# Last projection in four passes instead of two halves, its successor's factors and weights prepared inside it, and the feed-forward without loops

## The chip, the cores and the metric

One core of one Trainium2 chip runs the whole program. The metric is the device time of one execution in microseconds (us): 3321.41 us for the kernel before, the median of 3 runs (3314.15 to 3323.13). The change touches the last two of the kernel's stages.

## What is computed

The reference is a two-layer gated cross-attention block over 2048 tokens (4 sequences of 512) of width 512. Only its end matters here:

```python
x = x + jnp.tanh(g_xattn[1]) * _L1_xattn_ref(_layernorm(x), ...)   # ends in a projection
x = x + jnp.tanh(g_ffn[1]) * _L1_ffn_ref(_layernorm(x), w_gate_up, w_down, norm_weight)

# the end of _L1_xattn_ref: catq is 2048 x 4096, wproj 512 x 4096
return jnp.einsum('bsi,oi->bso', catq, wproj) * (proj_in_scale * proj_w_scale)

def _L1_ffn_ref(x, w_gate_up, w_down, norm_weight):
    def rmsnorm(x, weight, eps=1e-5):
        return x * jax.lax.rsqrt(jnp.mean(x * x, -1, keepdims=True) + eps) * weight
    def activation_quant(x):
        scale = 127.0 / jnp.clip(jnp.max(jnp.abs(x), -1, keepdims=True), 1e-05, None)
        return jnp.clip(jnp.round(x * scale), -128, 127) / scale
    def weight_quant(w):
        scale = 1.0 / jnp.clip(jnp.mean(jnp.abs(w)), 1e-05, None)
        return jnp.clip(jnp.round(w * scale), -1, 1) / scale
    def bitlinear(x, w):
        return jnp.einsum('bsh,oh->bso', activation_quant(x), weight_quant(w))
    gate, up = jnp.split(bitlinear(rmsnorm(x, norm_weight), w_gate_up), 2, axis=-1)
    return bitlinear(jnp.square(jax.nn.relu(gate)) * up, w_down)       # hidden width 1408
```

The weights of the feed-forward are made ternary (-1, 0, 1), which needs the mean magnitude of the whole matrix first.

## The kernel before

The two stages stand in `l1_output_and_ffn` (L2825). Tokens are handled in 16 tiles of 128. Each stage has its own buffers and semaphores and ends with a barrier of all engines. PE, DVE, ACT, POOL and SP are TensorE, VectorE, ScalarE, GpSimd and SyncE; each runs its own list of instructions in order and waits on semaphores.

**Projection, `l1_output` (L2837).** The contraction of 4096 is cut into 32 slices (k). The tokens go in two halves of 8 tiles, each tile with a PSUM bank (`acc0` to `acc7`). For each half and slice, SP loads `cat16` (128 x 1024, bf16), ACT turns it into fp32r (L2901), and PE makes two products for each tile, with the high and the low part of the weight slice (L2917, L2918). In the first half SP also loads the weight slice `w_raw`, DVE makes `w_hi` (L2940) and POOL `w_lo` (L3004); both stay for the second half. The order of SP's first loads is: two scale constants (L2879, L2880), then cat and weight in turn (L2886, L2889). SP loads the residual `x3` (4 MB, L2891) at slice 24 of the first half. When a half is done, DVE handles its tiles one by one: scaled addition to `x3` (L2991), which frees the bank, then mean and variance (L2994, L2996). In the second half PE waits at each bank's first product for that tile's L2991.

Beside this the ternary weights are made: POOL issues the loads of 12 parts of the raw weights (`t_raw`, L3016) in the first 24 slices, DVE sums magnitudes (L2951). Between the two halves' tiles DVE has `limits` and then 12 parts of `ternary` (L2976, L2979), each of them loaded again (L3027) and stored to DRAM (`wguq`, `wdq`, L3030) by POOL. POOL's last act in the stage is to wait for these stores.

**Feed-forward, `l1_ffn` (L3038).** SP loads `w_gate_up` in four pieces (L3105), `norm_w` (L3106) and `w_down` (L3107). POOL works out, for all 16 tiles together, the factor and bias of the double normalisation (11 dependent operations, L3281 to L3291, two of them powers); ACT and DVE wait for all 11. Then each tile goes through: ACT `centre` (xa, L3183), POOL `weigh` (xb, L3261), DVE `scale` (a maximum over 512 and two small steps, L3197 to L3202), `round_add` (xr, L3206), `round_sub` (xi, L3211), PE transposes (pX), ACT copy (hT, L3164), then four quarters of PE `gate_up` (L3134), ACT relu and square (L3170, L3173), DVE `hidden` (L3218); then DVE `hidden_scale` (the long maximum over 1408, L3223, and three small steps), `hidden_round` (L3236), `hidden_int` (L3241), PE transposes (pT, L3142), ACT copy (qT, L3178, L3179), PE `down` (L3153), DVE `residual` (L3247), SP store. The order on each engine is set by `pipeline` (L31): a stage with lag l handles item s - l in step s, the stages of a step in the order of the list; there are 64 items, four quarters for each tile, and `at(q, f)` runs f in quarter q alone. Steps before the largest lag and the last ones are written out, those between are a loop of 8 steps (2 tiles) on every engine. PE's gate_up of quarter i waits until `hidden` of quarter i - 2 is done (two banks).

## Time and profile before

| | |
|---|---|
| median of 3 runs | 3321.41 us |
| profiled execution, its own time | 3319.0 us |
| its span, first to last instruction | 3317.3 us |
| TensorE's mean granted clock | 0.959 |
| busy: PE, DVE, ACT, POOL | 2961.9, 2408.8, 2094.6, 1360.3 us |
| projection: first product to end of the last | 2861.5 to 3102.9 us |
| feed-forward: first gate product to the end | 3131.7 to 3317.3 us |

Times in the rows are microseconds from the start of the span, durations too unless marked ns. PE's matmuls overlap, so the distance between two starts is what one costs; PEld is the loading of its stationary operand. An operand's name carries the prefix `k_` in these stages. In brackets behind a row: how long the engine sat idle before it, and what released it.

### The profile page before, as it was taken

The page shows a single profiled execution, that of the slowest core. Times are in us where ns is not written, and L with a number is a line of the kernel's source. Part 1 is how long each engine was busy: PE and PEld are TensorE (multiplying, and loading weights), DVE is VectorE, ACT ScalarE, POOL GpSimd, SP SyncE. Part 2 cuts the span into 40 slices and gives each one's busy share as a digit, 9 for nine tenths or more (in the row PEclk, how much of TensorE's full clock was granted, in tenths as well). Part 3 has the DMA queues.
Part 4 walks back from the last instruction along what each step waited for, and adds up shares of the span by engine and source line. Part 5 has one row for each costly group of instructions (what it writes and reads, how often), then busy time and mean ns, then how long its engine had stood idle before and what let it go on. Part 6 is the DMA issues. An engine that isn't in the chain of part 4 may idle for free. (4 is left out here: it accounts for less than half of the span.)

```text
span 3317.3 us, 57690 instructions
## 1 busy us (share of the span) xinstructions
PE 2961.9 (89%) x15542; PEld 2354.9 (71%) x15542; DVE 2408.8 (73%) x4802; ACT 2094.6 (63%) x4247; POOL 1360.3 (41%) x1667
## 2 busy tenths in 40 slices
PE   6849899588899969979999899999999999799677
PEld 4636666477788857758787688888888888678444
DVE  6759999656676658767666189999999999534387
ACT  3448888331566636556666488888888888322255
POOL 3400000413000048246676277777777776331131
PEclk9979999799899989989999999999999999899899
DMA  5776564413877759865666523222233221566200
GB/s 184 245 158 157 140 157 109 120 48 137 278 262 263 232 159 300 208 180 154 175 175 200 187 88 95 93 91 76 90 95 93 93 93 45 173 234 206 71 23 29
DMA packets 403247, 490.88 MB, mean 148 GB/s; under 512 B 36388, under 2 KB 251828, under 8 KB 403092
## 3 DMA queue, kind: packets, MB, share of 16 engines
q1 hardware_dynamic: 391140, 440.31, 44.8%
q0 software_dynamic: 11952, 48.78, 4.2%
q8 instruction: 63, 1.03, 0.1%
q14 instruction: 92, 0.75, 0.1%
HBM read 312.69 MB, written 176.31 MB: 147 GB/s over the span
## 5 line engine op out<-in xcount | busy, mean ns | idle before, releaser
L2814 POOL TENSOR_SCALAR h_probs<-h_exp,h_rowsum_inv 128x512 f32<-128x512 f32 x512 | 357.5, 698 | 273.9 <-PE h_pT L2662 256.4
L2742 DVE TENSOR_REDUCE h_neg_max<-h_scores 128x1 f32<-128x512 f32 x512 | 349.4, 682 | 141.8 <-PE h_scores L2654 141.4
L2704 ACT ACTIVATE h_exp<-h_scores,h_neg_max 128x512 f32<-128x512 f32 x512 | 356.0, 695 | 108.8 <-DVE h_neg_max L2742 100.6
L2755 DVE TENSOR_TENSOR h_probsT_lo<-h_pT,h_probsT_hi 128x512 fp32r<-128x512 f32 x512 | 348.3, 681 | 0.0
L2662 PE MATMUL h_pT<-ident,h_probs 128*128 128x128 f32 x2048 | 306.2, 272 | 0.9 <-POOL h_probs L2814 0.8
L2662 PEld LDWEIGHTS h_pT<-ident,h_probs 128*128 128x128 f32 x2048 | 253.1, 139 | 69.9 <-POOL h_probs L2814 2.3
L2713 ACT CAST h_probsT_hi<-h_pT 128x512 fp32r<-128x512 f32 x512 | 301.1, 588 | 0.9 <-PE h_pT L2662 0.9
L2917 PE MATMUL k_acc<-k_w_hi,k_cat 128*128 (+1 forms) x512 | 202.4, 395 | 19.5 <-ACT k_cat L2901 16.2
L817 ACT ACTIVATE b_probs<-b_scores,b_neg_max 128x512 f32<-128x512 f32 x256 | 180.5, 705 | 39.9 <-DVE b_neg_max L845 39.6
L845 DVE TENSOR_REDUCE b_neg_max<-b_scores 128x1 f32<-128x512 f32 x256 | 173.7, 679 | 38.7 <-PE b_scores L768 38.7
L2677 PE MATMUL h_pO<-h_probsT_hi,n_lo 128*128 128x512 f32 x512 | 201.5, 393 | 0.0
L2918 PE MATMUL k_acc<-k_w_lo,k_cat 128*128 (+1 forms) x512 | 201.3, 393 | 0.0
L2901 ACT CAST k_cat<-k_cat 128x1024 fp32r<-128x1024 bf16 x64 | 67.3, 1051 | 183.4 <-PE k_acc L2918 170.1
L826 ACT CAST b_probsT_hi<-b_pT 128x512 fp32r<-128x512 f32 x256 | 151.6, 592 | 44.5 <-PE b_pT L776 44.4
L2513 DVE TENSOR_TENSOR g_normed<-g_pQ,g_rstd 128x512 f32<-128x512 f32 x160 | 110.3, 689 | 95.2 <-PE g_pT L2418 95.2
L2543 POOL TENSOR_TENSOR g_rstd<-g_var_eps,neg_half 128x4 f32<-128x4 f32 x160 | 172.0, 1075 | 13.3
L852 DVE TENSOR_TENSOR b_probsT_lo<-b_pT,b_probsT_hi 128x512 fp32r<-128x512 f32 x256 | 174.0, 680 | 1.4 <-issue 1.4
L2801 POOL TENSOR_TENSOR n_lo<-n_raw,n_hi_second 128x512 fp32r<-128x512 f32 x128 | 165.3, 1292 | 0.0
L2462 ACT ACTIVATE g_out<-g_pT,head_ln_b,head_ln_w 128x512 f32<-128x512 f32 x160 | 124.5, 778 | 61.1 <-DMA lnT<-g_out 60.4
L776 PE MATMUL b_pT<-ident,b_probs 128*128 128x128 f32 x1024 | 159.9, 279 | 3.5 <-DVE b_probsT_lo L852 2.3
L768 PE MATMUL b_scores<-b_k_stack,b_q_stack 128*128 128x512 f32 x256 | 124.1, 486 | 40.9 <-DMA b_k_stack<-qk 39.2
L776 PEld LDWEIGHTS b_pT<-ident,b_probs 128*128 128x128 f32 x1024 | 122.6, 142 | 48.2 <-issue 8.9
(439 smaller groups left out, 9135.4 us busy)
## 6 DMA issues: line engine op xcount, KB each, us to landing
e_w_raw<-in_w SPq DMA_DIRECT2D x24, 1792.0 KB, 8.0
lnT<-g_out SPq DMA_DIRECT2D x160, 256.0 KB, 2.4
n_raw<-lnT SPq DMA_DIRECT2D x64, 512.0 KB, 5.2
e_w_raw<-in_w SPq DMA_DIRECT2D x24, 896.0 KB, 9.6
b_q_stack<-qk SPq DMA_DIRECT2D x64, 256.0 KB, 7.3
b_k_stack<-qk SPq DMA_DIRECT2D x64, 256.0 KB, 9.2
xq<-f_out SPq DMA_DIRECT2D x16, 1024.0 KB, 7.1
n_raw<-lnT SPq DMA_DIRECT2D x64, 256.0 KB, 5.3
```

Source lines behind the costliest of these rows:

```text
L776: last = nc.tensor.transpose(pT[r % TB][:, k], Pr[:, r % 4, bass.ts(k, P)], g["ident"][:])
L817: nc.scalar.activation(Pr[:, r % 4], pS[r % SB][:], ACT.Exp, bias=nmax[:, r % 4:r % 4 + 1], accum_out=rsum[:, h, q:q + 1]).then_inc(exp_do ...
L852: nc.vector.tensor_tensor(PTl[:, h, :, bass.ts(q, P)], pT[r % TB][:], PTh[:, h, :, bass.ts(q, P)], ALU.subtract).then_inc(lo_done.sem, 1)
L2662: last = nc.tensor.transpose(pT[r % 4][:, k], Pn[:, r % 4, bass.ts(k, P)], g["ident"][:])
L2677: nc.tensor.matmul(pO[h][:], vl, PTh[:, br * HPG + h, k], start=False, stop=(k == QT - 1)).then_inc(o_mm.sem, 1)
L2704: nc.scalar.activation(Pr[:, r % 4], pS[r % 2][:], ACT.Exp, bias=nmax[:, r % 4:r % 4 + 1], accum_out=rsum[:, r % 4:r % 4 + 1]).then_inc(ex ...
L2713: nc.scalar.copy(PTh[:, br * HPG + h, :, bass.ts(q, P)], pT[r % 4][:]).then_inc(hi_done.sem, 1)
L2742: v.tensor_reduce(nmax[:, r % 4:r % 4 + 1], pS[r % 2][:], axis=AX, op=ALU.max, negate=True).then_inc(nmax_done.sem, 1)
L2755: v.tensor_tensor(PTl[:, br * HPG + h, :, bass.ts(q, P)], pT[r % 4][:], PTh[:, br * HPG + h, :, bass.ts(q, P)], ALU.subtract).then_inc(lo_ ...
L2814: nc.gpsimd.tensor_scalar(Pn[:, r % 4], Pr[:, r % 4], rinv[:, r % 4:r % 4 + 1], 1.0, ALU.mult, ALU.mult).then_inc(norm_done.sem, 1)
L2917: nc.tensor.matmul(pA[j][:], lhsT, Wh[:, k].rearrange("p a d -> p (a d)"), start=first, stop=False)
L2918: ins = nc.tensor.matmul(pA[j][:], lhsT, Wl[:, k].rearrange("p a d -> p (a d)"), start=False, stop=last)
```

## The change

The projection (`l1_output`) goes through the tokens in four passes of 4 tiles. Passes 0 and 1 are interleaved slice by slice, so that each weight slice still serves 8 tiles when it comes; passes 2 and 3 follow one after the other, on banks 0 to 3 and 4 to 7. An item is one slice of one pass (128 x 512 of cat): 128 items, 8 products each, all written out without a loop. cat has 8 buffers before ACT's conversion and 4 behind. SP's first load is a weight slice, the scale constants come behind the second cat, `x3` at item 32 (slice 16 of the interleaved passes). At item 64 SP waits for all `w_lo` and loads `norm_w` into a free weight buffer. At item 112, in the middle of pass 3, SP waits for the ternary stores and loads `w_gate_up` for the feed-forward; the ternary work's buffers lie in that same memory. DVE's order is unchanged in kind: tiles 0 to 7, limits, 12 ternary parts, tiles 8 to 15, where tiles 8 to 11 now belong to pass 2 and 12 to 15 to pass 3.

After its last store POOL works out the output constants and, once 12 tiles have their variance, the row factors of tiles 0 to 11 (4 operations with one power, the two normalisations being joined algebraically). Those of tiles 12 to 15 are made in the feed-forward, behind POOL's first `weigh`. Nobody waits for them before `centre` of tile 12. `w_down` is still loaded at the start of the feed-forward.

In the feed-forward every engine's list is written out in full. `centre` moves from quarter 0 to quarter 3 of the tile before, behind the hT copy on ACT; `weigh`, `scale`, `round_add` and `round_sub` move with it: DVE has `scale` between `hidden_round` and the second `hidden`, `round_add` behind `hidden_int`, and `round_sub` behind `residual`. All other lags grow by one. The diff, cut:

```diff
+    TP = 4
+    PASSES = NT // TP
+    N = PASSES * CK
+    def item(n):
+        return (n % 2, n // 2) if n < 2 * CK else divmod(n, CK)
+    UW, UC, UX = 4, 8, 4
+    X3, MV, Wr = shared.x3, shared.meanvar, shared.w_raw
...
-    Cb = m.sb("cat16", [P, U, HT * P], BF16)
-    Ct = m.sb("cat", [P, 2, HT * P], F32R)
+    Cb = m.sb("cat16", [P, UC, TP * P], BF16)
+    Ct = m.sb("cat", [P, UX, TP * P], F32R)
...
+    flat = shared.w_gate_up[:].rearrange("p k c -> p (k c)")
+    Tr = flat[:, 0:4 * F1].bitcast(F32).rearrange("p (a c) -> p a c", a=2)
+    Lt = flat[:, 4 * F1:5 * F1]
+    Tq = flat[:, 5 * F1:7 * F1].rearrange("p (a c) -> p a c", a=2)
...
+        def load_cat(n):
+            p, k = item(n)
+            if n >= UC:
+                sp.wait_ge(c_conv, n - UC + 1)
+            sp.dma_start(Cb[:, n % UC], t["cat"][k * P:(k + 1) * P, p * TP * P:(p + 1) * TP * P]).then_inc(c_in[n % UC], 16)
+        def load_w(k):
+            if k >= UW:
+                sp.wait_ge(w_lo, k - UW + 1)
+            sp.dma_start(Wr[:, k % UW], t["wprojT"][k * P:(k + 1) * P, :]).then_inc(w_in[k % UW], 16)
+        for n in range(N):
+            if n < 2 * CK and n % 2 == 0:
+                load_w(n // 2)
+            load_cat(n)
+            if n == 1:
+                sp.dma_start(sc[:, 0:1], t["proj_in_scale"].partition_broadcast(P)).then_inc(s_in, 16)
+                sp.dma_start(sc[:, 1:2], t["proj_w_scale"].partition_broadcast(P)).then_inc(s_in, 16)
+            if n == CK:
                 sp.dma_start(X3[:], t["x2"].rearrange("(n p) d -> p n d", p=P)).then_inc(x_in, 16)
-        segments(sp, [CK, CK], U, [(load, 0)], straight_end=CK // 2)
+            if n == 2 * CK:
+                sp.wait_ge(w_lo, CK)
+                sp.dma_start(shared.norm_w, t["norm_w"].partition_broadcast(P)).then_inc(shared.nw_in, 16)
+            if n == 3 * CK + CK // 2:
+                for r in range(2):
+                    sp.wait_ge(t_stored[r], 16 * NP // 2)
+                for k in range(KT):
+                    sp.dma_start(shared.w_gate_up[:, k], t["wguq"][k * P:(k + 1) * P, :]).then_inc(shared.gu_in, 16)
     @block.scalar
     def _(act):
-        def convert(seg, i, r):
-            n = i * U + r
-            act.wait_ge(c_in[r], i * 16 + 16)
-            act.wait_ge(mm.sem, mm.free(n))
-            nc.scalar.copy(Ct[:, r % 2], Cb[:, r]).then_inc(c_conv.sem, 1)
-        segments(act, [CK, CK], U, [(convert, 0)])
+        for n in range(N):
+            act.wait_ge(c_in[n % UC], 16 * (n // UC + 1))
+            if n >= UX:
+                act.wait_ge(mm, n - UX + 1)
+            nc.scalar.copy(Ct[:, n % UX], Cb[:, n % UC]).then_inc(c_conv, 1)
     @block.tensor
     def _(pe):
...
+        for n in range(N):
+            p, k = item(n)
+            pe.wait_ge(c_conv, n + 1)
+            if p == 0:
+                pe.wait_ge(w_lo, k + 1)
+            for j in range(TP):
+                bank = pA[p % 2 * TP + j]
+                if k == 0 and p >= 2:
+                    pe.wait_ge(x3_done, (p - 2) * TP + j + 1)
+                lhsT = Ct[:, n % UX, bass.ts(j, P)]
+                nc.tensor.matmul(bank[:], lhsT, Wh[:, k], start=(k == 0), stop=False)
+                ins = nc.tensor.matmul(bank[:], lhsT, Wl[:, k], start=False, stop=(k == CK - 1))
+                if k == CK - 1 and j < TP - 1:
+                    ins.then_inc(acc_done, 1)
+            ins.then_inc(mm, 1)
...
+        def tile(n):
+            p, j = divmod(n, TP)
+            if j < TP - 1:
+                dve.wait_ge(acc_done, p * (TP - 1) + j + 1)
+            else:
+                dve.wait_ge(mm, max(p + 1, 2) * CK - (p == 0))
...
+        for k in range(CK):
+            high(k)
+            if k % 2 and k // 2 < NP:
+                abs_sum(k // 2)
+        dve.wait_ge(summed, NP)
+        v.tensor_reduce(tot[:, 0:1], asum[:, 0:GP], axis=AX, op=ALU.add).then_inc(t_link, 1)
+        v.tensor_reduce(tot[:, 1:2], asum[:, GP:NP], axis=AX, op=ALU.add).then_inc(t_link, 1)
+        dve.wait_ge(s_in, 32)
+        v.tensor_tensor(gs[:, 0:1], sc[:, 0:1], sc[:, 1:2], ALU.mult).then_inc(s_done, 1)
+        dve.wait_ge(s_done, 1)
+        v.tensor_tensor(gs[:, 1:2], gs[:, 0:1], g["tanh_gates"][:, 1:2], ALU.mult).then_inc(s_done, 1)
...
-            if n == HT:
+            if n == 2 * TP:
                 limits()
                 for part in range(NP):
                     ternary(part)
...
+            tile(n)
...
+        shared.chain(pool, nc.gpsimd.tensor_scalar(shared.out_const[:, 0:1], g["w_mean"][:, 1:2], 1.0 / INT8, 1.0, ALU.mult, ALU.mult))
+        shared.chain(pool, nc.gpsimd.tensor_tensor(shared.out_const[:, 1:2], shared.out_const[:, 0:1], g["tanh_gates"][:, 3:4], ALU.mult))
+        pool.wait_ge(mv_done, shared.EARLY)
+        shared.row_factors(nc, g, pool, 0, shared.EARLY)
...
-        return i * 2 + r // CH, r // CH, r % CH
+        n, c = divmod(i * N + r, CH)
+        return n, n % 2, c
...
-        for k in range(KT):
-            sp.dma_start(Wg[:, k], t["wguq"][k * P:(k + 1) * P, :]).then_inc(gu_in, 16)
-        sp.dma_start(nw[:], t["norm_w"].partition_broadcast(P)).then_inc(nw_in, 16)
...
-        pipeline(sp, N, U, [(at(3, store), 0)])
+        pipeline(sp, N, N, [(at(3, store), 0)])
...
-        pipeline(pe, N, U, [(gate_up, 8), (down_part, 15), (at(3, h_transposes), 11), (at(3, x_transposes), 4)])
+        pipeline(pe, N, N, [(gate_up, 9), (down_part, 16), (at(3, h_transposes), 12), (at(3, x_transposes), 5)])
...
         def centre(n, b):
+            if n == shared.EARLY:
+                act.wait_ge(shared.rows_done, 2)
             act.wait_ge(xb.sem, xb.free(n))
...
-        act.wait_ge(pre, 11)
-        pipeline(act, N, U, [(at(3, qT_copy), 12), (relu_square, 8), (at(3, hT_copy), 4), (at(0, centre), 0)])
+                                 bias=sbias[:, bass.ds(n, 1)], scale=srow[:, bass.ds(n, 1)]).then_inc(xa.sem, 1)
...
-        dve.wait_ge(pre, 11)
-        pipeline(dve, N, U, [(at(3, hidden_scale), 9), (at(3, hidden_round), 10), (at(3, hidden_int), 11),
-                             (at(3, residual), 16), (at(1, round_add), 4), (at(2, round_sub), 4), (at(3, scale), 0),
-                             (hidden, 8)])
+        pipeline(dve, N, N, [(at(3, hidden_scale), 10), (at(3, hidden_round), 11), (at(3, hidden_int), 12),
+                             (at(3, residual), 17), (at(3, round_add), 4), (at(3, round_sub), 5), (at(3, scale), 3),
+                             (hidden, 9)])
...
             pool.wait_ge(xa.sem, xa.done(n))
+            if n == 0:
+                pool.wait_ge(shared.nw_in, 16)
             pool.wait_ge(xr.sem, xr.free(n))
-            nc.gpsimd.tensor_tensor(Xb[:, b], Xa[:, b], nw[:], ALU.mult).then_inc(xb.sem, 1)
+            nc.gpsimd.tensor_tensor(Xb[:, b], Xa[:, b], nw, ALU.mult).then_inc(xb.sem, 1)
+            if n == 0:
+                shared.row_factors(nc, g, pool, shared.EARLY, NT)
...
-        var = MV[:, :, 1:2].rearrange("p n a -> p (n a)")
-        steps = (
-            lambda: nc.gpsimd.tensor_scalar(row[:, 0], var, EPS, 0.0, ALU.add, ALU.add),
...
-        for k, step in enumerate(steps):
-            step().then_inc(pre, 1)
-            pool.wait_ge(pre, k + 1)
-        pool.wait_ge(nw_in, 16)
-        pipeline(pool, N, U, [(at(0, weigh), 0), (at(3, cubes), 1), (at(3, out_factor), 10)])
+        pipeline(pool, N, N, [(at(3, weigh), 2), (at(3, cubes), 3), (at(3, out_factor), 11)])
...
+    def row_factors(self, nc, g, pool, a, b):
+        mean, var = (self.meanvar[:, a:b, j:j + 1].rearrange("p n a -> p (n a)") for j in range(2))
+        c = slice(a, b)
+        self.chain(pool, nc.gpsimd.tensor_scalar(self.row[:, 0, c], var, 1.0 + EPS, EPS * EPS, ALU.mult, ALU.add))
+        self.chain(pool, nc.gpsimd.tensor_tensor(self.factor[:, c], self.row[:, 0, c], g["neg_half"][:, 0:b - a], ALU.pow))
+        self.chain(pool, nc.gpsimd.tensor_tensor(self.row[:, 1, c], mean, self.factor[:, c], ALU.mult))
+        nc.gpsimd.tensor_scalar(self.bias[:, c], self.row[:, 1, c], -1.0, 0.0, ALU.mult, ALU.add).then_inc(self.rows_done, 1)
```

## Rows read from the trace of the kernel before

**Rows 1.** Busy time by stretch: us, PE, PEld, DVE, ACT, POOL, PEclk, DMA share, GB/s
```profile
2980.00:3000.00 20.00, 16.71 (x57) 11.51 (x56) 15.19 (x28) 3.69 (x4) 2.50 (x4) 0.83 0.35 108
3103.00:3127.00 24.00, 0.00 (x0) 0.00 (x0) 9.07 (x19) 1.52 (x2) 8.02 (x12) 0.59 0.39 145
```

**Rows 2.** Timeline of the projection's start: start, length, engine, line, operation
```profile
2851.69 0.34 SPq L2879 DMA_DIRECT2D k_scales<-in_proj_in_scale  x1
2853.43 0.34 SPq L2889 DMA_DIRECT2D k_w_raw<-in_wprojT  x1
...
2861.48 0.76 PE L2917 MATMUL k_acc<-k_w_hi,k_cat 128*128 128x512 f32 x1 [16.22 <-ACT k_cat L2901]
```

**Rows 3.** The tile k_acc, and the timeline near the end of the first half
```profile
L2917 PE MATMUL k_acc<-k_w_hi,k_cat x512: 389/389/794, 2861.5 to 3102.2; 128*128 x128, 128*128 128x512 f32 x43
...
2975.86 1.05 ACT L2901 CAST k_cat<-k_cat 128x1024 fp32r<-128x1024 bf16 x1 [2.58 <-PE k_acc L2918]
2976.42 0.75 DVE L2991 SCALAR_TENSOR_TENSOR k_x<-k_acc,k_gated_scale,k_x 128x512 f32<-128x512 f32 x1 [13.69 <-PE k_acc L2918]
```

**Rows 4.** Timeline from the projection's last tiles to the first gate product
```profile
3099.72 0.75 DVE L2991 SCALAR_TENSOR_TENSOR k_x<-k_acc,k_gated_scale,k_x 128x512 f32<-128x512 f32 x1 [50.51 <-PE k_acc L2918]
...
3112.30 0.18 DVE L2996 BATCH_NORM_AGGREGATE k_meanvar<-k_bnstat 128x2 f32<-128x6 f32 x1
3113.53 0.31 POOL L3281 TENSOR_SCALAR k_row_scale<-k_meanvar 128x16 f32<-128x16 f32 x1 [63.47 <-POOLq L121]
...
3115.49 2.17 SPq L3105 DMA_DIRECT2D k_w_gate_up<-wguq  x4
...
3122.33 1.52 ACT L3183 ACTIVATE k_xa<-k_x,k_row_bias,k_row_factor 128x512 f32<-128x512 f32 x2 [25.64 <-POOL k_row_bias L3291]
3126.92 2.49 POOL L3261 TENSOR_TENSOR k_xb<-k_xa,k_norm_w 128x512 f32<-128x512 f32 x2 [4.62 <-DMA k_norm_w<-in_norm_w]
...
3129.02 0.15 DVE L3200 TENSOR_SCALAR k_act_step<-k_amax 128x1 f32<-128x1 f32 x1
...
3131.70 1.36 PE L3134 MATMUL k_gate<-k_w_gate_up,k_hT 128*128 128x352 bf16 x4 [0.68 <-ACT k_hT L3164]
```

**Rows 5.** Timeline of one tile in the feed-forward's loop, from gate to gate
```profile
3196.24 0.77 PE L3134 MATMUL k_gate<-k_w_gate_up,k_hT 128*128 128x352 bf16 x4 [0.94 <-ACT k_hT L3164]
...
3199.57 1.79 POOL L3261 TENSOR_TENSOR k_xb<-k_xa,k_norm_w 128x512 f32<-128x512 f32 x1 [7.41 <-ACT k_xa L3183]
...
3200.15 1.50 DVE L3206 TENSOR_SCALAR k_xr<-k_xb,k_act_scale 128x512 f32<-128x512 f32 x1
...
3204.23 0.67 DVE L3197 TENSOR_REDUCE k_amax<-k_xb 128x1 f32<-128x512 f32 x1
...
3206.71 1.62 DVE L3223 TENSOR_REDUCE k_amax<-k_hidden 128x1 f32<-128x1408 f32 x1
...
3207.16 0.77 PE L3134 MATMUL k_gate<-k_w_gate_up,k_hT 128*128 128x352 bf16 x4 [0.83 <-ACT k_hT L3164]
```

**Rows 6.** The same near the end, written out, with neither weigh nor scale
```profile
3283.39 0.77 PE L3134 MATMUL k_gate<-k_w_gate_up,k_hT 128*128 128x352 bf16 x4 [0.68 <-ACT k_hT L3164]
...
3285.82 0.52 DVE L3218 TENSOR_TENSOR k_hidden<-k_relu,k_up 128x352 f32<-128x352 f32 x1 [0.41 <-ACT k_relu L3173]
...
3287.12 0.48 DVE L3206 TENSOR_SCALAR k_xr<-k_xb,k_act_scale 128x512 f32<-128x512 f32 x1
...
3289.05 0.79 PE L3142 MATMUL k_pT<-ident,k_hidden_int 128*128 128x128 bf16 x11 [0.17 <-DVE k_hidden_int L3241]
...
3293.04 0.77 PE L3134 MATMUL k_gate<-k_w_gate_up,k_hT 128*128 128x352 bf16 x4 [0.68 <-ACT k_hT L3164]
```

**Rows 7.** Loads of the projection, KB and median us to landing; POOL's last store
```profile
k_w_raw<-in_wprojT SPq DMA_DIRECT2D x32, 256.0 KB, 4.4
...
k_x<-x SPq DMA_DIRECT2D x1, 4096.0 KB, 14.1
...
3049.51 0.55 POOL L3030 DMA_DIRECT2D wdq<-k_ternary  x1 [5.25 <-DVE k_ternary L2979]
```

227 lines of the change are left out of this document (84 added, 143 removed).

## The prediction, made before the changed kernel ran

> **What bounds the kernel now.** I read the busy time by stretch first, for where PE stands idle; then the timeline at the edges of the two stages; then one tile of the feed-forward. The projection is bound by PE: 1024 products [rows 3], and ACT's conversions follow PE at 1.05 + 2.58 = 3.63 us for 16 products, so one costs 0.2267 us and all 232.1 us. PE takes from 2861.48 to 3102.9, 241.4 us. Of the 9.3 us above, 1.6 are eight first products at half clock (0.425 us in place of 0.227, the granted clock still low), the rest, 7.7, lies between the halves: DVE needs about 1.6 us for a tile (8 tiles in 3112.48 - 3099.72 = 12.8, [rows 4]), PE only 0.453, so PE waits at the banks, and the granted clock of that stretch is 0.83 [rows 1]. Then PE is idle from 3102.9 to the feed-forward: DVE's tiles to 3112.48, POOL's factors until ACT starts at 3122.33, the wait for norm_w, which stands behind 2.8 MB of weights in SP's queue, until 3126.92, and the chain to the first gate at 3131.70 [rows 4]. Then 16 tiles, one each 10.92 us [rows 5], with DVE's xr on the path: 1.50 us while POOL weighs, 0.48 without [rows 5, 6].
>
> **The change part by part.**
>
> Start. Before the first weight slice SP issues two scales and one cat; it starts at 2851.69 and comes to the slice at 2853.43 [rows 2]. Now the slice is first: 1.7 us at least. From its issue to PE's first product passed 8.05 us, of which its cast and POOL's subtraction are about 1.9, so it landed after 6.1; its like land after 4.4 in the median [rows 7]. If the slice alone in front does too, 1.7 more. Bounds: 1.7 gained, and 4.5 (also without the start flags). I take 3.0. The second slice may still be late, but eight slow products stand before it.
>
> Middle. DVE starts tile 0 at the same place, 3.1 us before the last product of the interleaved passes [rows 3]. Bank j is free 0.75 + 1.6j us later (0.8, 2.3, 3.9, 5.5). PE is there at 3.2 + 0.45j, as a whole item of the other four banks (8 x 0.2267 = 1.81 us) lies between: 3.2, 3.6, 4.1, 4.5. Only tile 3 is late, by 1.0 us; pass 3's banks are free long before. A wait this short should leave the clock up. Gained 7.7 - 1.2 = 6.5; at worst the clock drops for some us (4 gained). Between passes 2 and 3 nothing waits: DVE is in the ternary parts, but those banks are not used.
>
> Tail of the projection. DVE has four tiles behind the last products in place of eight: 4 x (1.58 - 0.45) = 4.5 us less. DVE is free by then: its ternary ends some 10 us into pass 3.
>
> Front of the feed-forward. Old: from DVE's end 3112.48 to the gate, 19.2 us. New: barrier 1.05 (to POOL's 3113.53), centre 0.76, weigh 1.25, small hand-offs 0.3, then from the end of the first weigh to the gate as before 3131.70 - 3128.17 = 3.5: in sum 6.9. Gained 12.3. Bounds: if ACT's flag comes only with SP's first issue (3115.49, behind all start flags) 10.4; nothing is left that could give more than 13. The 11 POOL operations are covered by pass 3; those for tiles 12 to 15, at most the old 4 us, run while PE makes tile 0 and delay POOL's second weigh, which DVE needs only some 7 us later.
>
> Feed-forward. The tile period where everything is written out, POOL silent and DVE without scale, is 3293.04 - 3283.39 = 9.65 us, and there the pT transposes wait 0.17 us for hidden_int [rows 6]: the chain gate, relu, first hidden, rounding, xr, second hidden, hidden_int, pT, qT, down, pX, hT, gate sets it. In the new order xr leaves that stretch (0.5) and scale enters it: 0.67 [rows 5] and two small steps of about 0.15 [rows 4] with hand-offs, 1.1 us. So 9.65 + 1.1 - 0.5 = 10.25. Where is POOL? centre ends 0.8 us after the gate, weigh runs from 0.8 to 2.1, the long maximum from -0.45 to 1.2 [rows 5], its small steps to 1.8, rounding begins at 2.9 (hidden at 2.43, [rows 6]). So weigh meets only the small steps. Three cubes behind scale on POOL may touch hidden_int for 0.2. 15 periods: 15 x 10.25 = 153.8 against 3293.04 - 3131.70 = 161.3, 7.5 us gained. Bounds: 0 (period stays) and 16.6 (15 x 9.65). The last tile is as before.
>
> Do the small steps wait for weigh? The first act_step, a scalar operation on one column, ran at 3129.02 for 0.15 us in the middle of two weighs that held POOL from 3126.92 to 3129.41 [rows 4], whereas the wide xr took 1.50 beside one. So I cost it at nothing. The Trainium skill, "SBUF — State Buffer", section "Who interferes with whom", says that DVE's tensor_scalar may take the port pair shared with GpSimd, exclusively, and that whoever issues first blocks the other wholly; that fits xr, and taken literally the small steps of the hidden scale too would wait for weigh; by the row they do not, and by the page's word the sum would be some 5 us smaller, which is in rival 1.
>
> DMA. SP's wait at item 112: SP gets there when PE has done item 100, 9 us into pass 3. The last ternary store is issued at 3049.51 in the old time, 3046.5 in the new, lands about 5 later (4.4 for 256 KB, [rows 7]), 16 us into pass 3, which starts near 3035.3. Then four issues, and the weights take at most 11.4 us (3115.49 to 3126.92, norm_w behind them included, [rows 4]); cat 113 lands near 28. PE has work until 17 x 1.81 = 30.8. So it is hidden, with 2 to 3 us to spare. x3 comes at slice 16, beside t_raw loads, where before it came after them: 14.1 us [rows 7] against a stock of 12 items, 21.8 us. Hidden too, with about as much to spare.
>
> **Sum.** 3.0 + 6.5 + 4.5 + 12.3 + 7.5 = 33.8. The profiled execution took 3319.0 (span 3317.3), 2.4 below the median shown: 3319.0 - 33.8 = 3285.2, I say 3285 us.
>
> **Rivals.** A difference under 0.3% (10 us) is about what a measurement of this kernel cannot tell from none.
>
> 1. The tile period hardly falls: weigh blocks the small steps (they end at 2.7, hidden moves from 2.4 to 2.8, 0.4 x 14 = 5.6 us), or the new chain through weigh, scale and second hidden is tighter than I drew it, up to the old 10.92. For it: pT already waits for hidden_int. Against: act_step. Time 3285 + 5 to 8 = 3290 to 3293. Chance 0.17.
> 2. PE starves in the projection, at item 113 or behind x3. For it: the margins are 2 to 3 us of DMA time. Against: PE never starved in the old one, x3 in it. 3 to 8 us, half clock after it included: 3288 to 3293; with rival 1 up to 3300. Chance 0.13.
> 3. It does not do what it says at the edge: ACT starts centre only after SP's start flags, and the first slice lands no sooner: 1.9 + 1.3 less, 3288. Inside my own range.
> 4. Slower than before: code written out must be fetched. The feed-forward has 16 x 58 products and as many weight loads on PE, the projection 2048. If each new block of code stopped PE as long as a small load takes to land, 4.4 us, it would take 34 / 4.4 = 8 stops to eat the gain and 10 for a measurable loss; 15 stops give 3285 + 66 = 3351. Against: the end of the old feed-forward is written out and its only waits have names [rows 6]. It decides from 10 stops on. Chance 0.03.
>
> **How the numbers follow.** My forecast has 0.64; the cases within 0.3% (several shortfalls at once, above 3311) 0.03, rival 4 0.03. Everything else is faster by over 0.3%: 0.94. The range reaches down for a period near 9.9 and the best start (5 + 1.5 less, and some noise of the runs) to 3275, and up to rivals 1 and 2 together, 3300.
>
> **What would show it.** PE's first product near 2858.5; no wait between passes above 1.5 us and granted clock 1.00 there; projection's last product near 3093; xb starting 2 us after DVE's last variance, gate 7 us after it; k_xr at 0.48 throughout and gates 10.25 apart; PE idle on k_cat in pass 3 below 1 us. A k_xr still near 1.5, gates 10.9 apart, waits for k_cat by DMA, or idle PE put down to issue would make it wrong.

## The result and the profile after

The changed kernel took 3281.68 us (median of 4 runs, 3272.32 to 3285.97), the kernel before, on the same chip, 3320.9 us (4 runs). The ratio is 0.9881, with a 95% interval from 0.9865 to 0.9897. I had said 3285 us, between 3275 and 3300.

The profiled execution took 3272.32 us, of which the span is 3270.6. In it the stages ahead of the change, which are the same program, were 8.2 us shorter than in the profile of before, so spans can't be compared whole. I cut the time from attention's last operation on DVE (its start) to the end at four places. All experiments are read by the same cuts.

| us | to the first product | products | to DVE's end | to the first gate | first gate to the end | in all |
|---|---|---|---|---|---|---|
| before | 13.8 | 241.4 | 9.6 | 19.2 | 185.6 | 469.6 |
| after | 8.1 | 236.2 | 5.1 | 6.7 | 175.0 | 431.2 |
| gained | 5.7 | 5.2 | 4.5 | 12.5 | 10.6 | 38.4 |
| predicted | 3.0 | 6.5 | 4.5 | 12.3 | 7.5 | 33.8 |

The start, in the timeline of after (start, duration, what; the rows of before are [rows 2]):

```profile
2839.42 0.42 DVE L1789 TENSOR_TENSOR h_cat<-h_o_clipped,h_magic 128x512 bf16<-128x512 bf16 x1
...
2842.84 0.34 SPq L2890 DMA_DIRECT2D k_w_raw<-in_wprojT  x1
...
2843.35 0.65 POOL L3019 DMA_DIRECT2D k_w_gate_up<-in_wguT  x1 [12.57 <-POOLq L121]
...
2845.61 0.43 DVE L2942 CAST k_w_hi<-k_w_raw 128x512 fp32r<-128x512 f32 x1 [5.76 <-DMA k_w_raw<-in_wprojT]
...
2846.13 1.26 POOL L3011 TENSOR_TENSOR k_w_lo<-k_w_raw,k_w_hi 128x512 fp32r<-128x512 f32 x1 [2.13 <-DVE k_w_hi L2942]
...
2847.54 0.77 PE L2930 MATMUL k_acc<-k_w_hi,k_cat 128*128 128x512 f32 x1 [10.52 <-POOL k_w_lo L3011]
```

SP's first act is the slice, 3.4 us after attention's operation (5.8 before); DVE starts to cast it 2.8 us later, where before 6.1 passed from issue to cast. The load of POOL's beside it carries the name `k_w_gate_up` because the raw weights now lie in that tile.

The change of banks, in the timeline of after, and the busy time by stretch (per engine, with the number of instructions; then PE's granted clock, the DMA engines' share, GB/s):

```profile
2966.80 0.39 PE L2931 MATMUL k_acc<-k_w_lo,k_cat 128*128 128x512 f32 x1
2967.22 0.50 PE L2930 MATMUL k_acc<-k_w_hi,k_cat 128*128 128x512 f32 x1
...
2968.80 0.50 PE L2930 MATMUL k_acc<-k_w_hi,k_cat 128*128 128x512 f32 x1 [0.85 <-DVE k_x L2980]
```

```profile
2962.00:2970.00 8.00, 7.13 (x30) 5.28 (x30) 6.47 (x13) 2.25 (x4) 0.00 (x0) 1.00 0.22 67
```

Products start 0.227 us apart. Two gaps stand out: 0.42 ahead of tile 2 (0.2 late) and 1.25 ahead of tile 3 (1.0 late), 1.2 in all, and the clock stays at 1.00, where it was 0.83 at the change of halves [rows 1].

The front of the feed-forward, in the timeline of after (before: [rows 4]):

```profile
3088.70 0.18 DVE L2985 BATCH_NORM_AGGREGATE k_meanvar<-k_bnstat 128x2 f32<-128x6 f32 x1
...
3090.03 0.81 ACT L3189 ACTIVATE k_xa<-k_x,k_row_bias,k_row_factor 128x512 f32<-128x512 f32 x1 [12.80 <-SPq L152]
...
3090.93 1.26 POOL L3267 TENSOR_TENSOR k_xb<-k_xa,k_w_raw 128x512 f32<-128x512 f32 x1 [46.34 <-ACT k_xa L3189]
...
3091.58 0.38 SPq L3111 DMA_DIRECT2D k_w_down<-wdq  x1
...
3095.62 1.36 PE L3138 MATMUL k_gate<-k_w_gate_up,k_hT 128*128 128x352 bf16 x4 [0.68 <-ACT k_hT L3168]
```

The row factors are there, POOL waits for ACT alone, and only `w_down` is still to be issued. ACT starts 1.55 us ahead of SP's first issue: of the row of start flags that SP sets (L152, which the row names) it waits for its own, one of the first, and not for the rest. (`norm_w` lies in a free weight buffer, so `weigh` reads it under the name `k_w_raw`.)

A tile of the feed-forward, the same view, and all 16 xr by their line (minimum, median, maximum in ns):

```profile
3154.25 1.62 DVE L3228 TENSOR_REDUCE k_amax<-k_hidden 128x1 f32<-128x1408 f32 x1
...
3155.28 1.27 POOL L3267 TENSOR_TENSOR k_xb<-k_xa,k_w_raw 128x512 f32<-128x512 f32 x1 [4.34 <-ACT k_xa L3189]
...
3155.90 0.21 DVE L3232 TENSOR_SCALAR k_clipped_max<-k_amax,k_cube 128x1 f32<-128x1 f32 x1
...
3156.35 0.21 DVE L3236 TENSOR_SCALAR k_hidden_scale<-k_max_inv,k_cube 128x1 f32<-128x1 f32 x1
...
3158.27 0.68 DVE L3202 TENSOR_REDUCE k_amax<-k_xb 128x1 f32<-128x512 f32 x1
...
3159.67 0.89 DVE L3246 TENSOR_SCALAR k_hidden_int<-k_hidden_rounding 128x1408 bf16<-128x1408 f32 x1
...
3159.76 0.84 POOL L3278 TENSOR_TENSOR k_cube<-k_cube 128x1 f32<-128x1 f32 x1
...
3160.47 0.48 DVE L3211 TENSOR_SCALAR k_xr<-k_xb,k_act_scale 128x512 f32<-128x512 f32 x1
```

```profile
L3211 DVE TENSOR_SCALAR k_xr<-k_xb,k_act_scale x16: 478/479/485, 3093.3 to 3241.0; 128x512 f32<-128x512 f32 x16
```

POOL's weigh (3155.28 to 3156.55) lies beside the long maximum and the two small steps, and neither small step is longer for it (0.21 us each, and 0.21 again at 3246.50, where POOL is silent); xr has POOL's weigh behind it and takes 0.48 in all 16 tiles. Tiles follow at 10.07 us (10.92 and 10.99 by turns in the loop before), and the loads of the weights in pass 3 cost PE nothing: in the stretch no wait of PE for a converted `cat` is listed, nor one of ACT for a load. The nearer escape was at `x3`, behind which the load of item 33 came late for ACT (timeline of after):

```profile
2907.27 0.62 ACT L2916 CAST k_cat<-k_cat 128x512 fp32r<-128x512 bf16 x1 [3.74 <-DMA k_cat<-cat]
```

PE came to this item at 2909.91, 2.0 us after the end of its conversion; three items later, and in pass 3, a conversion ends 4.6 us ahead of its products.

### The profile page after: what moved, and what is told of

It reads as the page before. It is cut to its first block and busy times, and to the rows that moved or that the text cites. A ratio compares the mean times of both kernels' runs of the same rounds, so it can differ in the third digit from the quotient of the medians.

```text
span 3270.6 us, 57041 instructions
## 1 busy us (share of the span) xinstructions
PE 2953.2 (90%) x15542; PEld 2349.0 (72%) x15542; DVE 2395.1 (73%) x4802; ACT 2107.6 (64%) x4311; POOL 1351.6 (41%) x1666
## 5 line engine op out<-in xcount | busy, mean ns | idle before, releaser
L2930 PE MATMUL k_acc<-k_w_hi,k_cat 128*128 128x512 f32 x512 | 201.0, 393 | 11.4 <-POOL k_w_lo L3011 10.5
L2931 PE MATMUL k_acc<-k_w_lo,k_cat 128*128 128x512 f32 x512 | 200.5, 392 | 0.0
L2916 ACT CAST k_cat<-k_cat 128x512 fp32r<-128x512 bf16 x128 | 79.3, 621 | 160.2 <-PE k_acc L2931 142.8
L757 POOL DMA_DIRECT2D rows<-b_zero x16 | 8.8, 548 | 359.1 <-PE b_scores L768 358.8
```

What stands on the lines that cost most here:

```text
L2930: nc.tensor.matmul(bank[:], lhsT, Wh[:, k], start=(k == 0), stop=False)
L2931: ins = nc.tensor.matmul(bank[:], lhsT, Wl[:, k], start=False, stop=(k == CK - 1))
```

## The experiments

Here are the same cuts for every kernel that ran, with the steady distance from one tile's first gate to the next one's (half the distance of two where a loop makes them alternate). The time is that of one execution, for before, after and the last kernel a median. The stages ahead end anywhere between 2839.4 and 2852.6 us, and the kernels ran on several chips, so the cuts carry the comparison, not the time. The first column scatters from 8.1 to 9.9 us between kernels with the same start: the slice is cast 2.7 to 3.5 us after its issue, and in four of them (old order, factors late, halves, scale aside) the first product waited for ACT's conversion of cat instead, which ended up to 9.8 us after attention's operation. The product stretch scatters by some 0.9 us with the number of slow products at its head (7 to 13). The last stretch scatters with the granted clock: over the first 7.4 us from the first gate it was 0.75 to 0.82 in most kernels and 0.59 to 0.66 in five (old order, halves, POOL's load later, scale aside, xr behind hidden). Where the feed-forward is that of after, such a late clock makes the first tile 9.4 or 9.5 us long in place of 8.6 to 8.9.

| us | first product | products | DVE's end | first gate | gate to end | tile | time |
|---|---|---|---|---|---|---|---|
| before | 13.8 | 241.4 | 9.6 | 19.2 | 185.6 | 10.96 | 3320.9 |
| after | 8.1 | 236.2 | 5.1 | 6.7 | 175.0 | 10.07 | 3281.7 |
| old order, straight | 8.9 | 236.2 | 5.1 | 6.7 | 182.0 | 10.51 | 3290.9 |
| new order, loops | 8.1 | 236.8 | 5.1 | 6.7 | 181.9 | 10.65 | 3289.6 |
| factors late | 8.4 | 236.8 | 5.1 | 11.1 | 175.1 | 10.07 | 3285.1 |
| loads late | 8.5 | 236.2 | 5.1 | 18.9 | 175.0 | 10.07 | 3292.8 |
| halves of eight | 9.9 | 241.5 | 9.6 | 6.7 | 177.0 | 10.07 | 3285.8 |
| start order of before | 13.5 | 237.0 | 5.1 | 6.7 | 175.1 | 10.07 | 3287.9 |
| the same, POOL's load later | 10.7 | 237.2 | 5.1 | 6.7 | 176.8 | 10.07 | 3288.9 |
| wait at item 96 | 8.2 | 255.4 | 5.1 | 6.7 | 175.0 | 10.07 | 3303.6 |
| scale aside | 9.4 | 236.1 | 5.1 | 6.7 | 169.2 | 9.65 | 3280.8 |
| x early | 8.8 | 236.5 | 5.1 | 6.7 | 163.8 | 9.33 | 3270.7 |
| fourth gate first | 8.6 | 236.2 | 5.1 | 6.7 | 151.3 | 8.73 | 3258.1 |
| xr behind hidden | 8.2 | 237.1 | 5.1 | 6.7 | 150.8 | 8.45 | 3257.3 |

**The order or the straight code?** The feed-forward changed in two ways. One run takes the new order away, one the straight code.

```diff
-        pipeline(dve, N, N, [... (at(3, round_add), 4), (at(3, round_sub), 5), (at(3, scale), 3), (hidden, 9)])
-        pipeline(pool, N, N, [(at(3, weigh), 2), (at(3, cubes), 3), (at(3, out_factor), 11)])
+        pipeline(dve, N, N, [... (at(1, round_add), 4), (at(2, round_sub), 4), (at(3, scale), 0), (hidden, 8)])
+        pipeline(pool, N, N, [(at(0, weigh), 0), (at(3, cubes), 1), (at(3, out_factor), 10)])
```

> Everything as in the changed kernel, but the feed-forward's engines go in the order of before (centre and weigh at a tile's first step, scale beside the last hidden of the tile before, round_add and round_sub at steps 1 and 2), still written out straight. Theory (xr beside POOL's weigh was the price): k_xr takes 1.50 us again in all tiles where POOL weighs, the tile period is 9.65 + (1.50 - 0.48) = 10.67 us and the 15 periods from the first gate to gate 15 about 158 to 160 us, 9 to 10 more than the 149.5 of the changed kernel. Rival (the loop with its register work was the price, the order is worth little): periods near 10.1, 15 of them at 150 to 152 us. The rest of the program as in the changed kernel.

```diff
-        pipeline(pe, N, N, [(gate_up, 9), ...])
+        pipeline(pe, N, U, [(gate_up, 9), ...])      # U = 8 steps to a turn of the loop, on every engine
```

> The new order of the feed-forward, but in loops of 8 steps as before in place of straight code. Theory: the order carries most of the gain and the loop costs about 0.25 us a tile (10.92 in the old loop against 9.65 + 1.02 = 10.67 worked out for straight code), so k_xr stays at 0.48, periods are about 10.3 us and 15 of them 153 to 154 us (149.5 in the changed kernel). Rival (straight code carries it): periods 10.7 or more, 160 us and over. Second rival (a loop costs nothing): 149.5 to 150.5.

xr of the first and of the second kernel, by their line:

```profile
L3211 DVE TENSOR_SCALAR k_xr<-k_xb,k_act_scale x16: 479/1495/1499, 3104.9 to 3258.4; 128x512 f32<-128x512 f32 x16
```

```profile
L3211 DVE TENSOR_SCALAR k_xr<-k_xb,k_act_scale x16: 478/480/487, 3103.6 to 3258.2; 128x512 f32<-128x512 f32 x16
```

The old order brings the 1.50 us back, in straight code too, and a tile takes 10.51; the new order in loops has xr at 0.48 and 10.65. Each alone, against before, gives 3.6 or 3.7 us of the stage; both together give 10.6. Neither theory was whole: over the 15 periods (a period is the distance from one tile's first gate to the next one's) I had the order at 9 to 10 us and it is 7.6 (157.1 against 149.5), and the loop at 4 and it is 7.0 (156.5). In the column from gate to end they are 7.0 and 6.9.

These totals hold something that is not order. In the second tile the granted clock fell for some 3.4 us in the profile of before (0.57 in 3148 to 3152) and in that of the old order (0.57 in 3123 to 3127), and not in after or in the new order in loops. That tile took 12.04 us in before, over a steady 10.96, and 11.71 in the old order, over 10.51. So some 1.1 us of the 10.6 and 1.2 of the 7.0 went with the clock; between two kernels with the feed-forward of after such a fall made 1.2 us too (11.2 against 10.1, below). The steady distances are free of it: 10.96, 10.51, 10.65 and 10.07.

Where the loop's time goes is seen along the chain of one tile, 10.71 us in the loop and 10.07 in straight code. For example, from the end of the reduction `k_amax` to the start of `k_act_step` there are 0.13 us in the loop, 0.03 in straight code.

```profile
3171.99 0.68 DVE L3202 TENSOR_REDUCE k_amax<-k_xb 128x1 f32<-128x512 f32 x1
...
3172.80 0.15 DVE L3205 TENSOR_SCALAR k_act_step<-k_amax 128x1 f32<-128x1 f32 x1
```

The rows are the loop's; after has 3158.27 + 0.68 = 3158.95 and `k_act_step` at 3158.98. Counted from the tile's first gate, the first hidden part starts at 2.71 (2.43 in straight code), `k_act_step` at 4.82 (4.44), `k_hidden_int` at 5.55 (5.13), qT's copy at 7.39 (6.89), hT's at 10.00 (9.43) and the next gate at 10.71 (10.07). The operations last as long in both; the 0.64 us are hand-offs, each up to 0.20 us longer, and 0.28 of them lie ahead of the first hidden part.

**The front: factors or loads?** One kernel computes constants and all row factors at the feed-forward's start, one issues the loads there.

```diff
-        pool.wait_ge(mv_done, shared.EARLY)
-        shared.row_factors(nc, g, pool, 0, shared.EARLY)
...
+        shared.row_factors(nc, g, pool, 0, NT)       # in l1_ffn, ahead of POOL's pipeline
```

> The two constants and the row factors of all 16 tiles are computed on POOL at the feed-forward's start in place of behind the twelfth tile; the loads stay early. Theory (loads and factors lay beside each other before, and either alone keeps its own part of the 12.5 us): one power of 128x16 at 2.93 us (half the old factors' 5.86), three short operations and two constants, 0.2 to 0.3 each with hand-offs of 0.1, 4.5 to 5 us in all: the first gate 11.2 to 11.8 us after DVE's end in place of 6.7. Rival (POOL's factors are hidden beside something else): 6.7 to 8 us.

```diff
-            if n == 3 * CK + CK // 2: ... w_gate_up; if n == 2 * CK: ... norm_w
+        for k in range(KT):                          # in l1_ffn, ahead of w_down
+            sp.dma_start(Wg[:, k], t["wguq"][k * P:(k + 1) * P, :]).then_inc(shared.gu_in, 16)
+        sp.dma_start(nw, t["norm_w"].partition_broadcast(P)).then_inc(shared.nw_in, 16)
```

> w_gate_up in four loads, norm_w and w_down are issued at the feed-forward's start in the order of before; the row factors stay early. Theory (of the 12.5 us at the front, the late norm_w alone would take nearly all): SP's first issue comes 2.7 us after DVE's end, norm_w lands 11.4 later as before, then 4.8 to the first gate: the gate 18.5 to 19 us after DVE's end (6.7 in the changed kernel, 19.2 before), the time 12 us longer, although the row factors are ready. Rival (part of the factors' 8.8 us on POOL was on the path beside the loads): gate at 10 to 15 us.

The timeline of the kernel with late loads:

```profile
3098.33 0.81 ACT L3186 ACTIVATE k_xa<-k_x,k_row_bias,k_row_factor 128x512 f32<-128x512 f32 x1 [12.80 <-SPq L152]
...
3102.02 0.44 SPq L3107 DMA_DIRECT2D k_w_raw<-in_norm_w  x1
...
3111.39 1.26 POOL L3264 TENSOR_TENSOR k_xb<-k_xa,k_w_raw 128x512 f32<-128x512 f32 x1 [57.87 <-DMA k_w_raw<-in_norm_w]
...
3116.08 1.36 PE L3135 MATMUL k_gate<-k_w_gate_up,k_hT 128*128 128x352 bf16 x4 [0.68 <-ACT k_hT L3165]
```

The loads came as expected and the factors 0.1 us under their range. Factors late cost 4.4 us (6.7 to 11.1; it is the new form of four operations, the old eleven were not tried with early loads), loads late 12.2 (6.7 to 18.9): of the 12.5 gained, 0.3 is left for the factors once the loads are late. They lay beside each other, and whoever had moved only the factors would have seen next to nothing.

**Passes of four or straight code?**

```diff
-    TP = 4
+    TP = 8          # two halves, pass p in the same eight banks; cat 4 deep, x3 at slice 16
```

> The last projection in two halves of eight tiles again, with the changed kernel's straight code, early loads and row factors (eight of them early). Theory (banks freed at 1.6 us a tile against 0.45 of PE are what the passes save): PE waits at the banks between the halves some 7 us and its granted clock drops, products take 241 to 243 us in place of 236.2, and DVE ends 9.6 us after the last product in place of 5.1: together 10 us more, and 1 to 2 more for the eight row factors left for the feed-forward, if at all. Rival (straight code or the new start of the loads brought the 5 us of the projection, not the passes): products at 236 to 238 us with only the 4.5 at the tail lost.

Busy time of this kernel around the change of halves:

```profile
2969.00:2990.00 21.00, 17.80 (x63) 13.00 (x64) 16.14 (x27) 3.91 (x4) 2.49 (x4) 0.84 0.42 143
```

The stretch at the change of halves has the granted clock of before (0.84, [rows 1]: 0.83), the products take 241.5 us and the tail 9.6: straight code gives the projection nothing, the passes all of it. The rest of the gate-to-end column (2.0 more) is not the eight factors. The kernel with POOL's load later has 1.8 more and no such factors; in both the granted clock rose late in the first tile and fell again in the second (for 3122.5 to 3126.5 here, 0.58, behind 1.7 us in which PE waited for `k_hidden_int`), and that tile took 11.2 and 11.3 us. The same view of that stretch:

```profile
3122.50:3126.50 4.00, 3.92 (x21) 2.65 (x23) 1.14 (x3) 1.73 (x3) 0.42 (x2) 0.58 0.00 0
```

After and the four other kernels with its feed-forward have the same wait of 1.7 us without the fall. Why it fell in two executions of the seven stays open.

**The start.**

```diff
+            if n == 0:
+                sp.dma_start(sc[:, 0:1], ...); sp.dma_start(sc[:, 1:2], ...)
+            load_cat(n)
+            if n < 2 * CK and n % 2 == 1:
+                load_w(n // 2)
```

> SP issues the two scales and a cat load ahead of the first weight slice, as before; the rest as changed. Theory (the place of the slice in SP's queue is the gain at the start): from the last DVE operation of attention to the first product 1.7 to 5 us more than the 8.1 to 9.4 us of the changed kernel's kind, 10 to 13.8. Rival (the dropped start flags or the load's own scatter made the 5.7 us): 8 to 9.5 us, no difference.

The timeline of this start:

```profile
2848.64 0.42 DVE L1789 TENSOR_TENSOR h_cat<-h_o_clipped,h_magic 128x512 bf16<-128x512 bf16 x1
...
2852.04 0.34 SPq L2894 DMA_DIRECT2D k_scales<-in_proj_in_scale  x1
...
2852.55 0.65 POOL L3019 DMA_DIRECT2D k_w_gate_up<-in_wguT  x1 [12.53 <-POOLq L121]
...
2854.04 0.43 SPq L2890 DMA_DIRECT2D k_w_raw<-in_wprojT  x1
...
2860.22 0.43 DVE L2942 CAST k_w_hi<-k_w_raw 128x512 fp32r<-128x512 f32 x1 [11.16 <-DMA k_w_raw<-in_wprojT]
```

The old order alone gives 13.5 us, nearly the 13.8 of before. But the slice is issued only 2.0 us later (5.4 after attention's operation in place of 3.4) and lands 3.4 us later still (6.2 from issue to cast in place of 2.8). What differs is who is ahead: POOL's load of 704 KB stands 1.5 us ahead of the slice here (1.8 before), 0.5 us behind it in after. So one more run put POOL's load behind its first subtraction and left the rest.

```diff
-                load(part, part)
+                if k: load(part, part)
             low(k)
+            if k == 0: load(0, 0)
```

> The start order of before (scales and one cat ahead of the first weight slice), and POOL's first load of the ternary's raw weights (720 KB) issued behind its first subtraction in place of ahead of it. In the run with the old start order alone the slice landed 6.2 us after its issue (POOL's load stood 1.5 us ahead of it), in the changed kernel 2.8 us (0.5 us ahead of POOL's load). Theory (the slice waits behind POOL's load in the DMA engines): the slice lands 2.5 to 3.5 us after its issue and the first product comes 10 to 11 us after attention's last DVE operation, against 13.5 with the old order and 8.1 to 9.4 with the new. Rival (the scales and cat loads ahead of it in its own queue are what delays it): 6 us and 13 to 13.5 us again.

The timeline of that start:

```profile
2855.89 0.43 SPq L2890 DMA_DIRECT2D k_w_raw<-in_wprojT  x1
...
2859.28 0.43 DVE L2942 CAST k_w_hi<-k_w_raw 128x512 fp32r<-128x512 f32 x1 [8.36 <-DMA k_w_raw<-in_wprojT]
...
2861.00 0.65 POOL L3019 DMA_DIRECT2D k_w_gate_up<-in_wguT  x1
```

It lands after 3.4 us, which is inside the 2.7 to 3.5 of the kernels that issue it first, and the first product stands at 10.7. So the long landing goes with the other queue's large load ahead of it, 2.8 us of the start (13.5 to 10.7). Its place in its own queue is worth the 2.0 us of the issue; that leaves 8.7, inside the scatter of the new order. Each of the two runs is one execution.

**How near was the other side?** SP's wait for the ternary stores and the weight loads behind it, half a pass earlier:

```diff
-            if n == 3 * CK + CK // 2:
+            if n == 3 * CK:
```

> SP waits for the ternary stores and issues the four weight loads at item 96 in place of item 112, so all later cat loads stand behind that wait. Theory (the place of the wait in SP's queue sets whether it is hidden): SP comes to it before pass 3 begins, waits until the last store has landed some 15 us into pass 3, and cat 97 and the following come behind 2.8 MB of weights, some 25 us into pass 3 and more; PE has in stock the 8 items loaded and 4 converted, 12 to 13 of 1.81 us, 22 us in all. PE starves once, for 3 to 15 us, then starts at a lower granted clock, so the projection is 4 to 18 us longer (236.2 in the changed kernel). Rival (the queue is deep enough and the weights cost no DMA time that cat needs): no wait on converted cat over 1 us, projection at 236 us.

The timeline around its one long wait:

```profile
3045.45 2.08 SPq L2908 DMA_DIRECT2D k_w_gate_up<-wguq  x4
...
3055.43 2.18 ACT L2916 CAST k_cat<-k_cat 128x512 fp32r<-128x512 bf16 x4 [22.59 <-DMA k_cat<-cat]
...
3056.10 0.80 PE L2930 MATMUL k_acc<-k_w_hi,k_cat 128*128 128x512 f32 x1 [16.72 <-ACT k_cat L2916]
```

The busy time just after it:

```profile
3057.00:3061.00 4.00, 4.00 (x11) 3.03 (x11) 0.00 (x0) 1.22 (x3) 0.00 (x0) 0.50 0.48 147
```

PE starves once, for 16.7 us, then runs at 0.50 of the clock for a while: 19.2 us in all (236.2 to 255.4), half of what the whole change brings, and 1.2 above my bound of 18. The theory holds and its worst case was too mild. The change's item 112 is what makes the load free.

**Further.** Behind weigh everything goes a tile later, so that scale stands beside the last hidden part.

```diff
-    (at(3, hidden_scale), 10) ... (at(3, round_add), 4), (at(3, round_sub), 5), (at(3, scale), 3), (hidden, 9)
+    (at(3, hidden_scale), 14) ... (at(3, round_add), 8), (at(3, round_sub), 9), (at(3, scale), 5), (hidden, 13)
```

PE's and ACT's stages follow by four steps, POOL's cubes by three.

> A variant to go further: everything behind weigh is one tile (four steps) later, so that DVE's scale stands at the end of a tile beside the last hidden and out of the stretch between the rounding and hidden_int. Theory (the period is the chain gate, relu, hidden, rounding, scale, xr's slot, hidden, hidden_int, pT, qT, down, hT, gate, with scale's 0.98 us on it): without scale there the period falls from 10.07 towards 9.65 - 0.54 + small steps = 9.1 to 9.5 us, 15 periods 137 to 143 us, minus one tile more of filling (about 3 us): in all 5 to 9 us below the changed kernel. Rival (DVE's own busy time or PE's is the bound by now): periods stay at 9.9 to 10.1 and the time at 3282 or above it by the filling.

5.8 us, at the low end of what was expected, by a period of 9.65, above it: with 0.98 us of scale off the stretch only 0.42 came off the tile. Another chain ends there by now. This kernel's timeline has it:

```profile
3191.98 0.79 PE L3146 MATMUL k_pT<-ident,k_hidden_int 128*128 128x128 bf16 x11 [0.17 <-DVE k_hidden_int L3246]
...
3194.48 0.59 PE L3157 MATMUL k_down<-k_w_down,k_qT 128*128 128x512 bf16 x2 [0.52 <-ACT k_qT L3183]
...
3195.98 0.77 PE L3138 MATMUL k_gate<-k_w_gate_up,k_hT 128*128 128x352 bf16 x4 [0.68 <-ACT k_hT L3168]
...
3198.41 0.52 DVE L3223 TENSOR_TENSOR k_hidden<-k_relu,k_up 128x352 f32<-128x352 f32 x1 [0.40 <-ACT k_relu L3177]
```

PE waits for ACT's copies of qT, then of hT, and DVE for relu behind them.

```diff
-  pe: (gate_up, 13), (down_part, 20), (at(3, h_transposes), 16), (at(3, x_transposes), 9)
+  pe: (gate_up, 13), (down_part, 21), (at(3, x_transposes), 8), (at(3, h_transposes), 16)
-  act: (at(3, hT_copy), 9)        dve: (at(3, round_add), 8), (at(3, round_sub), 9)
+  act: (at(3, hT_copy), 8)        dve: (at(3, round_add), 6), (at(3, round_sub), 7)
```

DVE's residual also moves, behind scale.

> A variant to go further than the one with scale aside (tile period 9.65): there PE still waits 0.52 us for qT, 0.68 for hT and 0.17 for hidden_int in a tile, and DVE 0.40 and 0.46 for relu's squares. Here xr and xi stand before the first two hidden parts, the x transposes ahead of pT, hT's copy behind the third relu and down's parts a step later, so that a tile's first gate follows the last gate of the tile before. Theory (the chain through hT was the bound): the period falls to 8.6 to 9.2 us, where DVE's or PE's 8.28 us of busy time with hand-offs bound it; 15 periods 129 to 138 us in place of 145, some 6 to 14 us less. Rival (the chain int, pT, qT, down with ACT's queue stays the bound, as qT's copies now stand behind hT's): 9.5 to 10 us, no gain.

5.4 us less, period 9.33, between what the theory and the rival had: hT is off the chain, but qT's copies now stand between PE's fourth gate part and its relu, and DVE waits (timeline of this kernel):

```profile
3194.12 0.79 PE L3146 MATMUL k_pT<-ident,k_hidden_int 128*128 128x128 bf16 x11 [0.19 <-DVE k_hidden_int L3246]
...
3196.57 0.75 DVE L3252 SCALAR_TENSOR_TENSOR k_x<-k_down,k_out_factor,k_x 128x512 f32<-128x512 f32 x1 [0.95 <-PE k_down L3157]
```

```diff
-  pe: (at(3, h_transposes), 16)    act: [(at(3, qT_copy), 17), (relu_square, 13), ...]
+  pe: (at(3, h_transposes), 17)    act: [(relu_square, 13), (at(3, qT_copy), 17), ...]
```

> On the variant with period 9.33 us: PE makes the fourth gate part before pT instead of behind it, and ACT the fourth relu before qT's copies. There DVE waited 0.95 us in each tile for PE's last down part, and the fourth hidden part stood at 1.65 us behind scale because relu followed qT. Theory (that chain is the bound): the fourth hidden part comes 0.5 us earlier and the period falls to 8.7 to 9.0 us, 15 periods some 5 to 9 us less. Rival (qT, now later by the fourth relu and gate, 1.2 us, holds down's first part and with it the residual): 9.3 or more.

The period is 8.73 as foreseen, and the 15 periods are 7.5 us shorter (136.2 to 128.7), inside the 5 to 9 expected. The other 5.0 of the 12.5 us lie behind the last tile's first gate (27.6 to 22.6), where the kernel ahead had lost 2.4; I had not counted them. One execution gave 3258.13 us. And xr is back at 0.90, as weigh still runs when it begins. In its timeline:

```profile
3201.54 1.27 POOL L3267 TENSOR_TENSOR k_xb<-k_xa,k_w_raw 128x512 f32<-128x512 f32 x1 [5.51 <-ACT k_xa L3189]
...
3202.19 0.90 DVE L3211 TENSOR_SCALAR k_xr<-k_xb,k_act_scale 128x512 f32<-128x512 f32 x1
```

```diff
-  dve: ... (at(3, round_add), 6), (at(3, round_sub), 7), ..., (hidden, 13)
+  dve: ... (at(3, round_sub), 7), ..., (hidden, 13), (at(3, round_add), 6)
```

> On the variant with period 8.73 us: there xr took 0.90 us in place of 0.48, as POOL's weigh (1.27) still ran for its first half. Here xr stands behind the tile's first hidden part, so that weigh ends before it, and xi a place later. Theory (xr beside weigh is paid for again, and DVE without an idle gap is now the bound): xr back at 0.48, first hidden part perhaps waiting 0.1 for relu, period 8.35 to 8.5 us; about 4 to 5 us less than the one look at 3258.1, so 3250 to 3256 as median, a ratio to the kernel before of 0.980 to 0.982. Rival (PE, busy 8.3 us a tile, or the chain through qT is the bound): period 8.7 and 3258 as median.

The timeline of this kernel at the same place:

```profile
3206.50 0.52 DVE L3223 TENSOR_TENSOR k_hidden<-k_relu,k_up 128x352 f32<-128x352 f32 x1
...
3206.94 0.48 DVE L3211 TENSOR_SCALAR k_xr<-k_xb,k_act_scale 128x512 f32<-128x512 f32 x1
```

Its busy time in the steady part of the stage:

```profile
3150.00:3220.00 70.00, 65.85 (x480) 41.33 (x486) 67.47 (x134) 52.20 (x101) 22.75 (x40) 1.00 0.08 31
```

Period 8.45 as expected, median 3257.3 us of 5 runs (3250 to 3256 expected), a ratio to before of 0.9804 (0.9788 to 0.982). It beats both kernels. DVE is busy 67.47 of 70 us, so another order of the same operations has little left to give. Against the kernel ahead of it only 0.5 us shows from gate to end: the steady tiles gain 0.28 each, but the first took 8.42 us in place of 7.26, at a clock of 0.62 against 0.82 in the first 7.9 us, and the stretch behind the last tile's first gate 24.3 in place of 22.6, at 0.81 against 0.93 from 11.4 us behind that gate on. With one profile of each, I can't say whether the order does that or the execution.

## Why the prediction was right

The sum was 33.8 us, the cuts give 38.4; the median is 3.3 us below the forecast and inside the range. No step pointed the wrong way. The start and the feed-forward gave 2.7 and 3.1 us more than I had counted, the middle 1.3 less. By its steps:

- **Start**, 3.0 predicted, 5.7 measured, above the bound of 4.5. The place, 1.7, is right: so much lay between SP's first issue and the slice (2.0 in the run with the old start order), and without start flags ahead SP's first issue comes 0.6 sooner besides (3.4 us after attention's operation in place of 4.0). The landing was mis-sized: I took a small load's median of 4.4 us [rows 7] as the best case, and it took 2.8 at most (up to 3.5 in other kernels). That median is of loads in a busy stretch; here none was ahead of it in either queue. The run with POOL's load later shows whose load it was.
- **Middle**, 6.5 against 5.2. The waits at the banks are as drawn (1.0 us at tile 3, 0.2 at tile 2, none between the other passes, clock 1.00). At the head 12 products in place of 8 ran at 0.43 us, 0.8 us more; that isn't the earlier start's doing, as kernels with the same start had 7 to 13. Another 0.6 is in two of my terms: by the distances between products, only 7.3 of the 7.7 us lay between the halves, and the change of banks costs 1.4 and not 1.2, as the product behind each gap is slower too (0.34 us in place of 0.23).
- **Tail**, 4.5 against 4.5; the run with halves gives all of it back.
- **Front**, 12.3 against 12.5, each of its parts within 0.3 us, and rival 3 (ACT held by all of SP's flags) did not come: ACT waits for one of the first.
- **Feed-forward**, 7.5 against 10.6. The small steps were not blocked by weigh: 0.21 us beside it, which speaks against rival 1. The period is 10.07, where I had 10.25, 2.6 us over 14 tiles: scale takes 0.98 (3158.27 to 3159.25; I had 1.1), xr's place was worth 0.54 (I had 0.5), and 9.65 + 0.98 - 0.54 = 10.09. Another 1.7 us was an error of my sum: it put 10.25 for all 15 distances against 161.3 measured, and the first of these is short in both kernels (8.67 before, 8.59 after). And 1.1 us of the 161.3 is the fall of the clock in the second tile of before, which I took for the stage's own. The run with scale aside shows that the sum for the period was in part lucky: with scale gone from the stretch 9.65 was left, not 9.1, so the pieces of the chain can't be added so freely. And that much of the gain hung on straight code (3.6 us alone, 6.9 beside the new order) was nowhere in my text, because I started from a tile that was already written out. From the last tile's first gate to the end it was 1.2 us longer than before (25.5 against 24.3), at a clock of 0.72 in the last 14.6 us, 0.81 before in the last 13.3.
- **Rival 2** (PE starves) did not come, though the run with the wait at item 96 shows that it was real: 16 of SP's items separate a free load from 19 us. At item 113 the margin was wider than the 2 to 3 us that I had worked out (ACT waited for no load there); behind x3 PE had 2.0 us left.
- **Rival 4** (code must be fetched) left no trace: no wait of PE is put down to it in the written-out stages, and straight code was 6.9 us faster than loops.

I leaned on the Trainium skill, "SBUF — State Buffer", section "Who interferes with whom", for the statement that DVE and GpSimd share a port pair exclusively and that the first to issue blocks the other. The runs agree for the wide operations in both directions (xr 1.50 and 0.90 beside weigh; POOL's third cube, a 128x1 step that takes 0.19 us like the two ahead of it when nothing wide runs beside, took 0.84 and ended 0.04 after DVE's `k_hidden_int`), and not for DVE's scalar steps on one column, which ran beside weigh in 0.21 us as they do alone.
